# Stage one's layer loop written out, a fused mask in the last stage, and another order of work in stages two and three

## What is computed

```python
x = x + _L0_attn_ref(_layernorm(x), ...)   # 6 layers: 16-head attention with a relative term, MLP of 512
x = x + _L0_ffn_ref(_layernorm(x), ...)    # mixture of 8 experts, top 1, and a shared expert, hidden 352
x = x + _L1_attn_ref(_layernorm(x), ...)   # Mamba block: convolution, 16 states, scan over 256 steps
x = x + _L1_ffn_ref(_layernorm(x), ...)    # 2 layers: 8-head attention in a window of 64, gated MLP
```

```python
q, k = l2norm(q) * qs, l2norm(k) * ksc
q, k = rotary_xpos(q, k)
sim = einsum('bhwid,bhwjd->bhwij', q * 8.0, k)
mask = (i < j) | (i > j + WINDOW) | (j == -1)
attn = softmax(where(mask, -finfo.max, sim))
```

## Time and profile before

| | |
|---|---|
| median of 3 runs | 2105.95 us |
| the profiled execution, its own time | 2107.55 us |
| its span, first to last instruction | 2105.7 us |
| instructions | 41779 |
| granted TensorE clock, mean | 0.952 |
| busy: PE, PEld | 1794.7 us (85%), 1338.0 us (64%) |
| busy: DVE, ACT, POOL | 1658.0 us (79%), 1617.9 us (77%), 1222.4 us (58%) |

### The profile page before, as it was taken

The page is one execution under the profiler, slowest core; times in us unless marked ns, Lnnn a source line. Parts: engine busy times, 40 slices in busy tenths (PEclk is TensorE's granted clock), DMA queues, the critical chain, the costliest instruction groups (busy, mean ns, idle before and its releaser), DMA issues. The chain is left out here.

```text
span 2105.7 us, 41779 instructions
## 1 busy us (share of the span) xinstructions
PE 1794.7 (85%) x9958; PEld 1338.0 (64%) x9958; DVE 1658.0 (79%) x4049; ACT 1617.9 (77%) x5245; POOL 1222.4 (58%) x2106
## 2 busy tenths in 40 slices
PE   1788988888889888888998589659994999999996
PEld 0576766666666666666777457246662777777775
DVE  2898999899989988989999332668885777777773
ACT  1798998789888988889989224389971788888884
POOL 1266777666667666667767434349883554444450
PEclk9999999999999999999999689769997999999999
DMA  2222222122112221212220220112222000000000
GB/s 77 76 76 75 75 89 72 71 72 86 67 68 87 76 69 68 89 67 70 90 73 31 83 98 30 31 50 101 91 80 78 1 1 2 1 1 1 1 1 21
DMA packets 75345, 120.96 MB, mean 57 GB/s; under 512 B 10536, under 2 KB 59952, under 8 KB 67872
## 3 DMA queue, kind: packets, MB, share of 16 engines
q1 hardware_dynamic: 65920, 109.91, 14.9%
q10 hardware_dynamic: 7920, 5.60, 1.0%
q0 software_dynamic: 1248, 2.59, 0.4%
HBM read 95.44 MB, written 24.20 MB: 57 GB/s over the span
## 5 line engine op out<-in xcount | busy, mean ns | idle before, releaser
L441 ACT ACTIVATE a_prob<-a_scores,a_negmax 128x256 f32<-128x256 f32 x1536 | 706.7, 487 | 116.7 <-DVE a_negmax L543 66.3
L543 DVE TENSOR_REDUCE a_negmax<-a_scores 128x2 f32<-128x512 f32 x768 | 518.8, 676 | 54.8 <-PE a_scores L677 50.8
L689 PE MATMUL a_heads<-a_prob,a_diag 128*128 128x256 f32 x1920 | 483.4, 392 | 27.4 <-POOL a_diag L332 27.3
L332 POOL TENSOR_TENSOR a_diag<-ident,a_rowinv 128x256 f32<-128x256 f32 (+1 forms) x384 | 277.8, 728 | 283.7 <-DVE a_rowinv L597 252.5
L689 PEld LDWEIGHTS a_heads<-a_prob,a_diag 128*128 128x128 f32 x1920 | 362.5, 197 | 85.3 <-POOL a_diag L332 38.5
L677 PE MATMUL a_scores<-a_spread,a_spread 72*128 72x256 bf16 x1536 | 270.5, 278 | 121.1 <-ACT a_prob L441 70.5
L441 ACT ACTIVATION_READ_ACCUMULATOR a_prob<-a_scores,a_negmax 128x1 f32 x1536 | 337.8, 220 | 0.0
L677 PEld LDWEIGHTS a_scores<-a_spread,a_spread 72*128 72x128 bf16 x1536 | 124.5, 98 | 254.0 <-ACT a_prob L441 157.4
L1474 DVE TENSOR_TENSOR_SCAN c_state<-c_decay,c_psD 128x1024 f32<-128x1024 f32 x64 | 146.1, 2285 | 35.6 <-PE c_psD L1591 35.0
L1307 POOL TENSOR_TENSOR c_du<-c_state,c_c_row 128x1024 f32<-128x1024 f32 x64 | 151.3, 2366 | 30.0 <-DVE c_state L1474 20.7
L1932 ACT ACTIVATE d_prob<-d_psS,d_bias,d_inv 128x128 f32<-128x128 f32 (+1 forms) x256 | 122.1, 487 | 27.7 <-DVE d_bias L2066 27.3
(11 more groups left out here) (295 smaller groups left out, 4122.2 us busy)
## 6 DMA issues: line engine op xcount, KB each, us to landing
a_spread<-a_split SPq DMA_DIRECT2D x48, 576.0 KB
a_spread<-a_split SPq DMA_DIRECT2D x144, 192.0 KB
a_split<-a_parts SPq DMA_DIRECT2D x48, 384.0 KB
c_c_row<-c_rows SPq DMA_DIRECT2D x32, 512.0 KB, 3.6
b_w<-in_b_w SPq DMA_DIRECT2D x1, 2816.0 KB, 14.3
a_w<-in_a_w ACTq DMA_DIRECT2D x10, 256.0 KB, 5.1
b_w<-in_b_w SPq DMA_DIRECT2D x1, 1536.0 KB, 17.3
d_wqkv<-in_d_wqkv SPq DMA_DIRECT2D x2, 768.0 KB, 5.9
```

What stands on the lines that cost most here:

```text
L332: g.tensor_tensor(diag[part % RING][:], ident[:].unsqueeze(1).broadcast_to([P, len(heads), P]), rowinv[part % RING][:, heads.start:heads.s ...
L441: ins = a.activation(prob[part % RING][:, c, :], psS[part % 2][:, c, :], ACT.Exp, bias=negmax[part % 2][:, c:c + 1], accum_out=rowsum[part ...
L543: v.tensor_reduce(negmax[part % 2][:, hs], psS[part % 2][:, hs, :], AX.X, ALU.max, negate=True).then_inc(s["negmax_ready"], 1)
L689: ins = p.matmul(psH[:, t, :], diag[part % RING][:, k, :], prob[part % RING][:, c, :], start=(j == 0 and k == 0), stop=(j == HG - 1 and c ...
```

## The change

Four edits. Stage one: `run` writes out all six layers, with constants for every wait value, and no register or branch is left in it. Stage two: the router's matmuls go group by group between the transposes, and the third expert product moves behind the row numbers. Stage three: the last two transposed groups move between the first x and z projections, and ScalarE takes the exponentials of the first two groups before the last `parts`. Stage four: the mask matmul is gone; the query table is negated, and VectorE adds the mask (now f32 and +1e25), scales by `inv`, writes back to PSUM and takes the minimum in one instruction per head, `tensor_tensor_reduce`; ScalarE's exponential has the constant scale -1.

```diff
-            for kind, lay, q, part in span(min(slots), LSLOTS):
-                do(kind, lay, lay, q, part)
-            with eng.Fori(1, LAYERS - 1) as l:
-                for kind, lay, q, part in span(STEADY * LSLOTS, (STEADY + 1) * LSLOTS):
-                    do(kind, l + (lay - STEADY), lay, q, part)
-            for kind, lay, q, part in span((LAYERS - 1) * LSLOTS, max(slots) + 1):
+            for kind, lay, q, part in span(min(slots), max(slots) + 1):
                 do(kind, lay, lay, q, part)
...
-                v.wait_ge(s["scores_ready"], 1)
+                v.wait_ge(s["scores_ready"], NG)
...
                 product(0)
                 product(1)
-                product(2)
...
                 v.tensor_copy(row_u[:], row[:]).then_inc(s["routed"], 1)
-
+                product(2)
...
+                turn_x(0)
+                turn_x(1)
                 p.wait_ge(s["const_in"], 144)
-                p.wait_ge(s["xnT_ready"], NG)
-                for t in range(T):
-                    ins = p.matmul(psO[0][:, t * EXPERTS:(t + 1) * EXPERTS], xnT[:, t * P:(t + 1) * P], router[:],
-                                   start=True, stop=True)
-                ins.then_inc(s["scores_ready"], 1)
+                for k in range(NG):
+                    route_scores(k)
+                    if k + 2 < NG:
+                        turn_x(k + 2)
...
                 for k in range(NG):
                     gate(k)
-                    if k >= 2:
-                        parts(k - 2)
+                    if k == 2:
+                        parts(0)
                     if k >= 1:
                         low_copy(k - 1)
-                low_copy(NG - 1)
-                parts(NG - 2)
-                for k in range(NG - 1):
+                parts(1)
+                exps(0)
+                low_copy(3)
+                exps(1)
+                for k in range(2, NG):
+                    parts(k)
                     exps(k)
-                parts(NG - 1)
-                exps(NG - 1)
...
                         project_x(k, t)
+                        if k == t == 0:
+                            for j in range(2, NG):
+                                turn_n(j)
                         project_z(k, t)
-                    if k == 0:
-                        for j in range(2, NG):
-                            turn_n(j)
...
-        maskf = sb("maskf", [P, L + P])
-        mask = sb("mask", [P, L + P], BF16)
-        identb = sb("identb", [P, P], BF16)
+        mask = sb("mask", [P, L + P])
...
-                                           bias=bias[n % 2][:, j:j + 1], scale=inv[q % 2][t][:, 0, h:h + 1],
+                                           bias=bias[n % 2][:, j:j + 1], scale=-1.0,
...
-                chain.link(v.tensor_copy(mask[:], maskf[:]))
-                chain.link(v.tensor_copy(identb[:], ident[:]))
...
-                        v.tensor_reduce(negmax[n % 2][:], psS[n % 2][:, :, k0:k1], AX.X, ALU.max, negate=True)\
-                            .then_inc(s["max_step"], 1)
-                        v.wait_ge(s["max_step"], n + 1)
                         v.wait_ge(s["inv_ready"], 2 * q + t + 1)
-                        v.tensor_tensor(bias[n % 2][:], negmax[n % 2][:],
-                                        inv[q % 2][t][:, 0, hh[0]:hh[1] + 1], ALU.mult)\
-                            .then_inc(s["bias_ready"], 1)
+                        for j, h in enumerate(hh):
+                            part = psS[n % 2][:, j, k0:k1]
+                            ins = v.tensor_tensor_reduce(part, part, mask[:, P * t + k0:P * t + k1],
+                                                         inv[q % 2][t][:, 0, h:h + 1], LARGEST, ALU.add, ALU.min,
+                                                         accum_out=bias[n % 2][:, j:j + 1])
+                        ins.then_inc(s["bias_ready"], 1)
...
-                        p.matmul(out, identb[:], mask[:, m0 + k0:m0 + k1].unsqueeze(1)
-                                 .broadcast_to([P, 2, k1 - k0]), start=True, stop=True)
-                        p.matmul(out, qT[q % 2][:, c, t * P:(t + 1) * P], kT[q % 2][:, c, :, k0:k1], start=False,
-                                 stop=True, skip_group_check=True).then_inc(s["s_full"], 1)
+                        p.matmul(out, qT[q % 2][:, c, t * P:(t + 1) * P], kT[q % 2][:, c, :, k0:k1], start=True,
+                                 stop=True).then_inc(s["s_full"], 1)
...
-    tab = np.stack([QK_SCALE * cos * scale, QK_SCALE * sin * scale, cos / scale, sin / scale])
+    tab = np.stack([-QK_SCALE * cos * scale, -QK_SCALE * sin * scale, cos / scale, sin / scale])
```

More of the change, by code:

```diff
@@ L1033, in _, with turn_x @@
             def _(p):
-                for k in range(NG):
+                def turn_x(k):
                     p.wait_ge(s["xn_ready"], k + 1)
@@ L1040, in _, with route_scores @@
                     ins.then_inc(s["turned"], 1)
-                p.wait_ge(s["const_in"], 144)
-                p.wait_ge(s["xnT_ready"], NG)
-                for t in range(T):
-                    ins = p.matmul(psO[0][:, t * EXPERTS:(t + 1) * EXPERTS], xnT[:, t * P:(t + 1) * P], router[:],
-                                   start=True, stop=True)
-                ins.then_inc(s["scores_ready"], 1)
+                def route_scores(k):
+                    p.wait_ge(s["xnT_ready"], k + 1)
+                    for t in range(k * TPG, (k + 1) * TPG):
+                        ins = p.matmul(psO[0][:, t * EXPERTS:(t + 1) * EXPERTS], xnT[:, t * P:(t + 1) * P], router[:],
+                                       start=True, stop=True)
+                    ins.then_inc(s["scores_ready"], 1)
+                turn_x(0)
+                turn_x(1)
+                p.wait_ge(s["const_in"], 144)
+                for k in range(NG):
+                    route_scores(k)
+                    if k + 2 < NG:
+                        turn_x(k + 2)
                 def hidden(i):
@@ L1665 @@
 NORM_MIN = 1e-12
-MASKED = -1e25
+MASKED = 1e25
+LARGEST = 3e38
 UNITS = DEPTH * SEQS
@@ L1750, in stage_d @@
         kT = [sb(f"kT{u}", [P, CD, 2, L]) for u in range(2)]
-        negmax = [sb(f"negmax{u}", [P, 2]) for u in range(2)]
         bias = [sb(f"bias{u}", [P, 2]) for u in range(2)]
@@ L1773, in stage_d @@
                  "o_full", "o_free", "square_ready", "rope_ready", "ss_ready", "inv_ready", "qk_ready", "pool_step",
-                 "max_step", "bias_ready", "rowinv_ready", "hn_ready",
+                 "bias_ready", "rowinv_ready", "hn_ready",
                  "gelu_ready", "mid_ready", "x_ready", "reduce_done")
@@ L1834, in _ @@
             def _(sp):
-                for dst, name in ((tables, "d_tables"), (maskf, "d_mask"), (down, "d_down")):
+                for dst, name in ((tables, "d_tables"), (mask, "d_mask"), (down, "d_down")):
                     sp.dma_start(dst[:], d[name]).then_inc(s["const_in"], 16)
```

1 line of the change is left out of this document (removed).

## The result

| | before | changed |
|---|---|---|
| median of the runs | 2105.56 us (4 runs) | 2056.60 us (2052.97 to 2060.75, 4 runs) |
| profiled execution, its span | 2107.55, 2105.7 us | 2058.43, 2056.5 us |

The ratio is 0.9763, interval 0.9744 to 0.9783: 49 us less, where 39.4 were forecast. The two traces place it. The borders are starts of single instructions; the last column is what the forecast gave that stretch.

The account below looks back on a forecast made before the run. No engine alone was at its limit; stages are chains through several engines, priced at the wait that ends last. Stage gains 22.4 + 3.3 + 3.7 + 10 = 39.4 us, and 1.6 for the profiled execution, took 2107.55 to 2066 us, range 2052 to 2080.

Parts of the forecast that it names:

- the pace of a written-out layer: Stage one: a written-out layer takes 181.38 us, as its written-out neighbours do; four cost 725.5 instead of 747.92, gaining 22.4 us.
- The jumps: Stage one: three jumps back of the layer loop, 3 x (74.97 - 70.22), cost 14.3 us of the 22.4 gain.
- The upper bound of 28: Stage one: gain of some 28 us if layer 0's five late passes hold waits that a middle layer lacks.
- The product's 2.1: Stage two: moving the third expert product behind the row numbers lets VectorE read the prefix counts 2.1 us earlier.
- The router's 1.2: Stage two: router matmuls placed between the transposes fill TensorE's gaps, gaining 1.2 us, bounds 0.8 to 1.5.
- TensorE's share: Stage four: mask matmuls are 1.05 us per unit of TensorE's chain; ScalarE's backlog lets only 0.72 be won.
- VectorE's extra: Stage four: the fused instructions change VectorE's time per score by -0.03 to +0.30 us, taken as +0.15.
- A: Rival, chance 0.17: the last stage gains nothing but setup, as ScalarE waits longer for the fused result; 2076 us.
- B: Rival, chance 0.13: all of TensorE's gain in the last stage arrives and stage one gives 26 us; 2055 us.
- C: Rival, chance 0.08: only the jumps pay in stage one (14.3 us), the scores' DRAM round trip limiting next; 2075 us.
- D: Rival, chance 0.03: slower, the fused instruction makes VectorE bound the last stage, each half about 0.9 us; 2140 us.
- E: Rival, chance 0.04: stage one's written-out loop gains nothing, fetching four times the code stalls as the jump did; 2089 us.

## Why the prediction was right or wrong

**Stage one: right cause, term too small** (22.4 forecast, 32.3 measured). The step that failed is the pace of a written-out layer, "111.57 + 69.81 = 181.38". Both neighbours that it was taken from held short falls of TensorE's clock. Of the 24 middle layers in the six traces with this code, six ran at a clock of 1.00 and took 177.2 to 177.7 us; at 0.98 they took 180.0 to 180.8, and the one at 0.96 184.4. The changed kernel's four average 179.5. That is 30.0 us instead of 22.4, and layers 0 and 5, which the edit leaves alone, gave 0.9 and 1.5 more in this execution. The jumps were priced at 4.75 each by passes that held such a fall as well (the trip without a jump back had one of 24.28 us); pass against pass they are 27.60, 27.70 and 28.15 against 21.87, so 5.9 each, 17.8 of the 30.0 (the three ran at a clock of 0.94, so some of it is the clock's). The upper bound of 28, for "waits of their own" in layer 0, was nearer than the value taken, and still short of the 30.0. That such falls also make the runs of the changed kernel lie 8 to 11 us apart is likely, but only profiled executions show a clock.

In one point the mechanism was misread, and it didn't matter for the sum: the forecast took ScalarE's 5.7 us for a wait on VectorE's maximum. It was ScalarE's own jump, and ScalarE's register work, not VectorE's, is what lengthens the other passes. To go by the trace's 5.7 us and not by the bare branch time was the right choice.

**Stage two: the product right, the router open** (3.3 forecast, 2.1 measured). The product's 2.1 came as 2.15 at the count copy. The router's 1.2 came as 0.4 in this execution: the step assumed that a gap closed on TensorE is passed on, and left out the clock, which rose later here than in the kernel before, so that the matmuls behind ran at the lower level for longer. In two executions of the same order where it rose 3 us sooner, more than the 1.2 arrived. "About 1 us later" for the fifth block was 1.95, and here a fall of the clock followed that the forecast didn't name; the two together used up the cover at the first packed rows and left 1.55 us of 3.81 at the second.

**Stage three: right.** 4.2 for the exponentials was 4.4; the transposes' cost of 0.5 didn't show.

**Stage four: right sum, wrong parts** (10 forecast, 10.4 measured). TensorE's share was capped as expected, but at 0.28 to 0.44 us per unit, not 0.72. VectorE's extra was 0.41 us per score, above the forecast's upper bound, because the read of an accumulator comes once per head and takes 142 ns; it cost 0.03 us per unit all the same, so the 0.15 charged for it was too much. The advice against fusing (the Trainium skill, "VectorE: DVE Perf Modes", Rules for kernel authors) is borne out for VectorE alone, which spends more, and not for the unit; the formula's 291 ns for the 128-column half was 356. What made up the difference is a term that the forecast lacked: the exponential's scale became a constant, which the diff shows in one line, and each got 90 ns cheaper. A list of what a change adds and removes has to include operands. The setup's 0.9 us showed as 0.25, counted from the last scan to the first clear.

**The rivals.** A (only the setup gains in stage four) fell: 0.74 us per unit came. B's number, 2055, is where the time lies, though not by its reasons: TensorE's gain did not arrive whole, and stage one gave 32, not 26. C fell, since the passes without a jump got shorter as well; the copy through DRAM shows in waits of 1.2 and 1.8 us, twice in a layer, and the kernel before stood 1.4 and 1.9 us at the same two places, so the shorter layer made them no longer. What they cost was not shown. D did not happen: each half is 0.50 us, or 0.57 at 192 columns, where it needed 0.9. The scan's 2285 ns per 1024 columns are 0.29 and 0.43 us for 128 and 192, not the "0.4 to 0.6" of the text, which changes nothing. E fell: compared layer by layer, a written-out one never ran slower than the looped one in its place.

## What to carry to other kernels

When a loop's body is long, price its jump on each engine by itself, by the pass that holds it against the pass that doesn't, at equal granted clock; the stalls of the engines overlap, and writing out the loop on the one engine whose stall is longest and which starts every step gets more than half of the gain. Where several engines jump together, a wait put down to a semaphore may be the waiting engine's own stall. Before an order of work is called worthless, look at every trace that has it: the same front of stage two gave 0.4 us in one and 2 in another. Read the operands of an unchanged instruction in a diff: a per-partition scale from a tile instead of a constant was worth as much here as a matmul.

## What the runs showed of the hardware

- A jump back over a layer's code took ScalarE 5.6 to 5.9 us, GpSimd 4.7 to 4.8, VectorE 2.9 to 3.3 and TensorE 2.7 to 3.3. All five together had thirteen packets of instructions in the 35 us around it, against five in the written-out code.
- ScalarE's exponential of 128 x 128 from PSUM took 369 ns with a constant scale and 457 with one from a tile, at 192 columns 423 and 518.
- VectorE's fused add, scale and minimum over 128 PSUM columns with write-back took 356 ns and its accumulator's read 142; 423 and 142 at 192 columns.
- TensorE's clock fell for moments in stage one in some layers and not in others of the same code; the layer took 177.2 to 177.7 us at 1.00 and 184.4 at 0.96. What starts a fall was not found: waits for the DRAM copy stood ahead of some and not of others, and the layers at 1.00 had the same waits.
- At the front of stage two the clock rose 13.1 to 16.4 us after the first transpose, in traces of the same code. Behind the same 1.95 us of standing TensorE's clock fell at once in two traces and did not in three.
- ScalarE stood up to 11.8 us beside GpSimd's scatters in one group of runs, with its input ready.
